# Where a unit's two halves of attention products stand in TensorE's order, in a kernel of deformable attention and a second attention

## The reference

```
x_ln = layernorm(x);  q = x_ln @ wq + bq
o = gelu(depthwise_conv7x7_stride2(q));  offsets = conv1x1(o)
grid = refs + tanh(offsets)             # 256 sampled points
interp = grid_sample_bilinear(x, grid)
v = k = interp @ wv + bv
qh, kh, vh = heads(q @ mq_w + mq_b), heads(k @ mk_w + mk_b), heads(v @ mv_w + mv_b)
attn = softmax(qh @ kh.T)               # 8 heads, 1024 queries x 256 keys
att = attn @ vh
z = att @ mo_w + mo_b + x
y = gelu(layernorm(z) @ mlp_w + mlp_b) + z
# second block, on y
theta, phi, g = y @ w_theta, maxpool(y @ w_phi), maxpool(y @ w_g)
out = y + sigma * (softmax(theta @ phi.T) @ g @ w_o)
```

## Time and profile before

| | |
|---|---|
| median of 3 runs | 526.87 us (522.64 to 527.66) |
| the profiled execution | 524.93 us |
| its span in the trace | 523.1 us |
| granted TensorE clock, mean | 0.964 |
| TensorE matmul, busy | 456.5 us (87%) |
| VectorE, busy | 286.2 us (55%) |
| ScalarE, busy | 211.7 us (40%) |
| GpSimd, busy | 120.6 us (23%) |
| TensorE's share of the chain that ended last | 64% |
| VectorE's | 11% |
| DMA's | 8% |
| ScalarE's, GpSimd's | 5%, 5% |

### The profile page before, as it was taken

The page is one execution under the profiler, slowest core; times in us unless marked ns, Lnnn a source line. Parts: engine busy times, 40 slices in busy tenths (PEclk is TensorE's granted clock), DMA queues, the critical chain, the costliest instruction groups (busy, mean ns, idle before and its releaser), DMA issues.

```text
span 523.1 us, 9272 instructions
## 1 busy us (share of the span) xinstructions
PE 456.5 (87%) x3727; PEld 320.2 (61%) x3727; DVE 286.2 (55%) x609; ACT 211.7 (40%) x336; POOL 120.6 (23%) x163
## 2 busy tenths in 40 slices
PE   0978988978599999998999999989989897988966
PEld 0956755645357666665687676656766574665734
DVE  3619433855555437847863375457546737537253
ACT  1112110555134333675416145655346474463340
POOL 5601200176001200375102000681012021100000
PEclk9998888999798999999999999999989998899989
DMA  7492885785804790157026920293117310000112
GB/s 209 92 207 43 187 127 104 127 197 70 117 0 59 101 235 7 59 90 111 9 82 101 184 34 2 82 121 63 43 42 102 62 42 1 2 3 1 41 41 82
DMA packets 30489, 42.90 MB, mean 82 GB/s; under 512 B 6075, under 2 KB 21230, under 8 KB 30446
## 3 DMA queue, kind: packets, MB, share of 16 engines
q1 hardware_dynamic: 23886, 35.08, 37.0%
q0 software_dynamic: 3584, 4.50, 3.2%
q10 hardware_dynamic: 2976, 2.73, 2.7%
HBM read 16.16 MB, written 4.19 MB: 39 GB/s over the span
## 4 chain that ended last, share of the span: by engine, by line
PE 64%; DVE 11%; DMA 8%; POOL 5%; issue 5%; ACT 5%; SPq 0%; ACTq 0%; DVEq 0%; POOLq 0%
PE ps_d L735 8%; PE ps_d L723 5%; PE ps_d L860 5%; PE ps_d L755 5%; PE ps_d L837 5%; PE ps_d L937 5%; PE ps_s L784 4%; PE ps_v L826 4%; PE ps_t L803 4%; PE ps_v L820 4%; DMA q_st<-mx_t 3%; PE ps_d L879 2%; DMA xa<-in_x_dram 2%; DVE mx L1560 2%; POOL samp L1871 2%
## 5 line engine op out<-in xcount | busy, mean ns | idle before, releaser
L1189 ACT ACTIVATE prob<-ps_t 128x1024 f32<-128x1024 f32 x64 | 65.4, 1022 | 102.3 <-PE ps_t L803 101.4
L1560 DVE TENSOR_REDUCE mx<-ps_s 128x4 f32<-128x1024 f32 x64 | 78.2, 1222 | 34.4 <-PE ps_s L784 33.3
L1843 POOL DMA_DIRECT2D q_st<-mx_t x64 | 34.1, 534 | 261.2 <-ACT mx_t L1181 244.8
L735 PE MATMUL ps_d<-cstack,conv_w 128*32 128x256 f32 x1024 | 59.9, 388 | 3.5 <-DMA cstack<-qpad 3.1
L784 PE MATMUL ps_s<-k_st,q_st 96*128 96x256 f32 x256 | 51.4, 325 | 8.5 <-DVE mx L1560 5.6
L803 PE MATMUL ps_t<-q_st,k_st 98*128 98x256 f32 x256 | 43.9, 295 | 12.7 <-DMA q_st<-mx_t 6.1
L735 PEld LDWEIGHTS ps_d<-cstack,conv_w 128*32 128x32 f32 x1024 | 35.7, 110 | 25.3 <-issue 6.2
L784 PEld LDWEIGHTS ps_s<-k_st,q_st 96*128 96x128 f32 x256 | 37.3, 198 | 21.7 <-DVE mx L1560 9.6
L803 PEld LDWEIGHTS ps_t<-q_st,k_st 98*128 98x128 f32 x256 | 36.7, 198 | 15.4 <-issue 7.7
L820 PE MATMUL ps_v<-prob,vh 128*32 128x256 f32 x512 | 36.2, 402 | 0.8 <-DVE att L1574 0.7
L1574 DVE TENSOR_TENSOR att<-ps_v,rden 128x256 f32<-128x256 f32 x32 | 13.6, 424 | 40.3 <-ACT rden L1200 40.2
(11 more groups left out here) (177 smaller groups left out, 751.0 us busy)
## 6 DMA issues: line engine op xcount, KB each, us to landing
q_st<-q_parts SPq DMA_DIRECT2D x42, 256.0 KB, 6.8
xa<-in_x_dram SPq DMA_DIRECT2D x8, 512.0 KB, 9.0
z_all<-in_x_dram SPq DMA_DIRECT2D x8, 512.0 KB, 9.2
out_dram<-z_all SPq DMA_DIRECT2D x8, 512.0 KB, 2.6
cstack<-qpad SPq DMA_DIRECT2D x22, 180.5 KB, 5.7
k_st<-cstack SPq DMA_DIRECT2D x24, 128.0 KB, 3.9
q_st<-z_all SPq DMA_DIRECT2D x6, 256.0 KB, 5.6
cstack<-att SPq DMA_DIRECT2D x6, 180.5 KB, 6.0
```

Source lines behind the costliest of these rows:

```text
L735: ins = pe.matmul(ps[32 * k:32 * k + 32, 0, :], conv_w[:, cb * 4 + k, y, x, :], cstack[:, cb, k, y:y + HG_, x:x + WG_], start=n == 0, stop ...
L1189: drain(act.activation(prob[:, u % 2, 2 * pr:2 * pr + 2].rearrange("p h m s -> p (h m) s"), ps_t[:], ACT.Exp), t_ring, "t", b, u, pr)
L1560: drain(dve.tensor_reduce(mx[:, u % 2, half, :], ps_s[:], AX.X, ALU.max), s_ring, "s", b, u, half)
```

## The change

On TensorE alone, `values_mixed` goes from its place behind `shifted(..., 0)` to the place of `values_summed` at the end of the slot, so that the two stand side by side. In slot two they stand side by side at the place that `values_mixed` had, and nothing is left of them at the slot's end. The tail stays as it was, as do the lists of the other engines and the semaphores they wait for.

```diff
@@ -954,8 +954,8 @@
                 if in_front(b, s, "off") and b == 0:
                     offsets(n)
-                if unit_of(b, s, 3):
-                    values_mixed(*unit_of(b, s, 3))
+                if unit_of(b, s, 3) and s == 2:
+                    values(*unit_of(b, s, 3))
                 if s == 0 and fin:
                     sums1(mm)
@@ -996,8 +996,8 @@
                 if unit_of(b, s, 2):
                     shifted(*unit_of(b, s, 2), 1)
-                if unit_of(b, s, 3):
-                    values_summed(*unit_of(b, s, 3))
+                if unit_of(b, s, 3) and s != 2:
+                    values(*unit_of(b, s, 3))
                 if in_front(b, s, "qh1") and b == 0:
                     queries(n, 1)
```

## The result

The changed kernel took 535.01 us, the median of 5 executions (532.39 to 539.64), against 526.87 of before (5 executions, 522.64 to 529.97): a ratio of 1.0196, with an interval of 1.0147 to 1.0245. On another chip it took 534.80 (6 executions) against 523.78 (25): 1.0191 (1.0143 to 1.0239). The medians are 8.1 and 11.0 us apart, the recorded ratios stand for about 10, and 535.01 is 10.1 above the 524.93 from which the forecast started: it added 5.3 to it. The median lies half a microsecond outside the range. The recorded ratios leave out executions that lie over 1.5% above the fastest of their kernel, while the means and the split further on use all of them.

What follows compares the result with a forecast made beforehand. The prediction took TensorE as busy most of the time, with VectorE pacing the middle of slots such as five. Profiled 524.93 us + 3.3 for order + 2.0 for clock = 530.2 us; range 525.5 to 534.5, holding about 0.8.

Steps and rivals of the forecast that it cites:

- The middle is paced by VectorE: Slot five: VectorE's reduction sets the second scores' start, so moving the products saves nothing there and costs 0.89 us at the end.
- Rival B: Slots four, five, seven: second scores start 0.9 us earlier, so the kernel gets faster, 518.6 us; chance 0.06.
- D: Whole kernel: gains and costs cancel, ScalarE's bank wait is 0, the clock is unchanged, 525.5 us; chance 0.12.
- slots two and three together: Later batches: sums fill slot two's wait, less a bank wait in slot three, -0.74 us for the two slots.
- The bank of slot three: Slot three: project products come earlier but wait for ScalarE to empty their bank, between 0 and 1.0 us, taken as 0.37.
- slot one: Slot one of batches two to four: mlp rows cover the middle, so only the join gains, -0.11 us each.
- The order's sum: All slots of the four batches: costs and gains of the new order together, +3.3 us, joins included.
- The 0.08 per join: TensorE's weight loads, 32 against 128 columns: the skill page's 0.08 us per join, 2.2 in all; the forecast kept 0.11, 3.0.
- The first batch's order: First batch, slots three to seven: later slot ends mostly vanish in the 6.09 us DMA wait, taken as +0.3 us.
- The idea that the row's DMA would gain room from later keys: First batch: keys' DMAs start some 2 us later and may leave the row's DMA more room, down to -1.3 us.
- the clock, +2.0 forecast: Longer gaps in bare slots of batches two to four bring falls to 1.2 GHz: at most 4.0 us, taken as +2.0.
- rival C: Every bare slot, the first batch's too, starts a 1.2 GHz stage and one delays the queries' DMAs: 533.9 us; chance 0.13.

Runs made afterwards that it cites:

- e7: The kernel of before with the products of values left out of slot five in batches two to four: 523.07 us (one execution).
- f3: The kernel of before with the changed order only in slots five to seven of the first batch: ratio 1.0059 to before.
- e1: The changed order in batches two to four, the first batch as before: 531.85 us against 525.09 of before, ratio 1.0102.
- e5: The kernel of before with the changed order in the first batch only: 529.68 us against 525.30, ratio 1.0082.
- f2: The kernel of before with the changed order only in slots three and four of the first batch: ratio 0.9999 to before.
- f1: The changed kernel itself, measured and profiled a second time: 534.80 us, ratio 1.0191 to before.
- e2: The changed kernel with products also run in their old place in the first batch and slots four, five, seven: 530.20 us, ratio 1.0108 to before.
- e6: The kernel of before with the first batch in changed order, its products run also in their old place: ratio 1.0076 to before.

## Why the prediction was too low

**The middle is paced by VectorE: right.** The step of 2.88 from the transposes to the second scores was 2.87 with the products moved, and 2.87 with them left out (e7). The waits for row maxima are 15.5 us ("over 12"). Rival B, which needed the second scores 0.9 earlier, is out, and so is D: slots two and three together came to -0.64, -0.94 and -0.88 for -0.74 each. The bank of slot three did cost something, which D needed to be nothing: the projection starts 0.77 behind the first `shifted` (196.26 to 197.03), where slot one's mlp rows, which wait for no bank there, start 0.48 behind it. That is about 0.3 for the 0.37 taken.

**The order's sum: right within what can be told.** The forecast was +3.3; the rest after the clock's part is +3.1 ± 0.9. By slots at full clock the second and third batches sum to +1.3 and +1.05 for 1.5 each. The difference is slot one, -0.38 and -0.45 for -0.11: from the first `shifted` to the mlp rows it is 1.63 us before (165.65 to 167.28) and 0.48 after (169.80 to 170.28), so taking the products out saves 1.15 there and not 1.00. The 0.08 per join that the forecast worked out from the Trainium skill (TensorE: Matmul & The Clock Gate, LDWEIGHTS), an estimate, would have been further off there still.

**The first batch's order: its sign right, its size short, its reason incomplete.** Forecast +0.3, from a step that read "behind them stands the wait of 6.09 us". Measured 1.6 ± 1.0 by the split. In the changed kernel's first profile, without a stage between slots five and seven, the way from slot five to the second batch takes 33.67 us; the eight profiles with the old order have 33.0 in the mean (32.2 to 33.6), before's 33.16: +0.5 to +0.7, which is inside the spread of the eight. The idea that the row's DMA would gain room from later keys, down to -1.3, did not come true: it took 9.72 us in the changed kernel and 9.71 before, though the keys' DMAs were issued 1.7 us later behind slot five's start (137.10 - 121.78 against 132.33 - 118.75). In f3, where they are issued from 140.08, as it lands, the release came 0.6 nearer to slot five, so some room may be there, but not 1.3. And the wait named in the trace was not the only one: VectorE's chain had 5.0 us to spare before, and 3.0 in the changed order.

**The step that failed: the clock, +2.0 forecast, +7.0 ± 2.9 measured.** The forecast listed the new gaps as "slot five of batches two and three" and "slots four and five of the fourth", and bounded them by 4.0. For these batches the runs show 3.7 ± 2.7 (e1), within that bound though not the 2.0 taken. What the list left out is the first batch, 3.4 ± 1.7 (e5). Most of it lies in slots five to seven, 2.2 ± 1.2 (f3); slots three and four have 1.0 ± 1.6 (f2), which may be nothing. Slots five and six have the largest gaps that the change made, 2.23 and 1.4 to 1.9, and they were counted as swallowed by the wait for the DMA. A gap is not swallowed when what it sets off is not: the clock stays low over the products, the sums and the keys, and these feed VectorE's chain, which had 3.0 us to spare. The order's term of that batch, 0.3 for a measured 1.6 ± 1.0, was short as well, by less. All this is part of rival C's condition ("the first batch's too"), and C's 533.9 was the nearest of the five times; but not every bare slot had a stage, and the queries' DMAs were not held up (in f1 and e5 the release comes 0.2 later behind slot five's start), so C's number was in part luck.

That it is the gaps, and not the order, which bring the clock down is shown by e2 and e6: the changed order with the gaps filled has the clock of before (parts of -1.1 ± 1.6 and 0.1 ± 1.4, against 7.0 ± 2.9 and 3.4 ± 1.7). Filling a gap also adds work for TensorE, and these runs do not tell the two apart. Which gap has a fall behind it is open. The gap of 1.54 in slot five of the second batch had none in the first profile and one in the second; the stages ahead of it, from the setup on, lie at other places in the two profiles, and no run here controls that.

## What to carry to other kernels

Work that stands in an engine's wait was free here, and it was also what kept the clock up: before moving it, price both, and count a new gap of the size that had a fall behind it here (1.4 to 2.2 us) as a possible stage at half clock, wherever it is. A long wait swallows a delay only up to the slack of the next releaser behind it, so follow the delay through all that the late piece feeds before writing it off. To tell order from clock, compare executions by their mean clock as well as their time, and try the order with the gap filled.

## What the runs showed of the hardware

**More work, less time.** e2 runs more matmuls than the changed kernel and takes less time (1.0108 of before, against 1.0191); e7 runs fewer and its slot five of batch three is 1.56 us longer.

**The price of lowered clock.** A microsecond of lowered time cost 0.69 us of span over all executions here; that the rest lies under waits is likely and not shown. Most stages took 1.7 us of lowered time (4 us with a mean of 0.57) or 3.4 (7 us with a mean of 0.52). Net of what later waits gave back, the stage behind slot five of the second batch cost 0.4 us (slots five to seven, +1.29 for +0.88).

**A small DMA.** The row's DMA of the maxima (4 KB) took 9.7 us in the first batch, with the queries' DMAs around it, where the median over the kernel is 1.9 us. It was 9.72 in the changed kernel and 9.71 before, with the keys' DMAs issued 1.7 us later behind slot five's start, and by the releases some 0.6 shorter in f3.
